# Regrouping nine of sixteen blocks of the last batch during its last pass instead of after it

## What is computed

```python
# per batch b of 8: x is 512 tokens x 2048 features, w = weight[itok[b]] is 2048 x 2048
c = einsum('bsi,boi->bso', x, w)                    # "cond", 4 streams of 512 columns
n = c * rsqrt(mean(c*c) + eps)
H_res  = g * sinkhorn((n @ W_res.T + base) / 0.1, 50 rounds) + (1-g) * I   # 4 x 4 per token
H_pre  = softmax(n @ W_pre.T + base)                # 4 per token
H_post = n @ W_post.T + base                        # 4 per token
y = (sum over j of H_pre[j] * c[stream j]) @ W_branch
out[stream i] = x[stream i] + sum over j of H_res[i, j] * c[stream j] + H_post[i] * y
```

## Time and profile before

| what | value |
|---|---|
| median of 3 runs | 1697.8 us (1697.26 to 1698.08) |
| the profiled execution's own time | 1699.75 us |
| its span | 1698.0 us |
| PE busy | 1685.5 us, 99% of the span |
| DVE busy | 1419.9 us, 84% |
| ACT busy | 717.7 us, 42% |
| POOL busy | 102.5 us, 6% |
| granted clock of TensorE | 1.000 of full speed |
| transfers | 255.55 MB, mean 151 GB/s |

### The profile page before, as it was taken

One profiled execution on the slowest core, in us unless ns is written; L12 is line 12 of the kernel. 1 busy time (PEld: TensorE's weight loads), 2 busy tenths in 40 slices (PEclk: granted clock), 3 DMA queues, 4 the chain that ended last, 5 costly groups with the idle time before them and its releaser, 6 DMA issues.

```text
span 1698.0 us, 24553 instructions
## 1 busy us (share of the span) xinstructions
PE 1685.5 (99%) x7758; PEld 1361.3 (80%) x7758; DVE 1419.9 (84%) x5964; ACT 717.7 (42%) x1171; POOL 102.5 (6%) x143
## 2 busy tenths in 40 slices
PE   9999999999999999999999999999999999999998
PEld 7888788887888878888788878888788877888785
DVE  4322499988999889998899978999799897998798
ACT  4333434244343443444334444334533443335672
POOL 0000000010000100001000000001000010001131
PEclk9999999999999999999999999999999999999999
DMA  6323424376334842448334572346622593227898
GB/s 241 99 88 124 149 88 112 101 216 193 100 100 115 240 166 87 112 130 265 114 95 116 161 249 98 88 126 220 214 88 89 145 300 136 95 92 207 228 217 218
DMA packets 69729, 255.55 MB, mean 151 GB/s; under 512 B 8032, under 2 KB 8160, under 8 KB 68704
## 3 DMA queue, kind: packets, MB, share of 16 engines
q1 hardware_dynamic: 49872, 182.16, 32.7%
q0 software_dynamic: 19728, 71.84, 17.8%
HBM read 204.16 MB, written 45.61 MB: 147 GB/s over the span
## 4 chain that ended last, share of the span: by engine, by line
PE 95%; DMA 2%; DVE 2%; ACT 1%; issue 0%; SPq 0%; DVEq 0%; ACTq 0%
PE acc L1278 79%; PE turn_ps L1315 3%; PE y_ps L1357 3%; PE logit_ps L1323 2%; PE logit_ps L1326 2%; PE acc L1441 1%; DMA w_raw<-wt 1%; PE y_ps L1391 1%; PE acc L1464 1%; PE y_ps L1441 1%; DMA piece<-xn 1%; DVE piece L1127 1%; PE acc L1304 1%; PE turn_ps L1335 0%; PE y_ps L1347 0%; PE acc L1503 0%
## 5 line engine op out<-in xcount | busy, mean ns | idle before, releaser
L1278 PE MATMUL acc<-w_hi,x_hi 128*128 128x512 f32 x2032 | 804.7, 396 | 1.8 <-ACT acc L564 1.8
L1278 PE MATMUL acc<-w_hi,x_lo 128*128 128x512 f32 x2032 | 792.8, 390 | 0.0
L1278 PE MATMUL acc<-w_lo,x_hi 128*128 128x512 f32 x2032 | 791.2, 389 | 0.0
L531 ACT ACTIVATE w_hi<-w_raw 128x1024 fp32r<-128x1024 f32 x255 | 269.2, 1058 | 443.6 <-DMA w_raw<-wt 443.4
L1278 PEld LDWEIGHTS acc<-w_hi,x_hi 128*128 128x128 f32 x2032 | 381.7, 188 | 82.0 <-DVE w_lo L876 2.8
L1278 PEld LDWEIGHTS acc<-w_hi,x_lo 128*128 128x128 f32 x2032 | 381.4, 188 | 81.9
L1278 PEld LDWEIGHTS acc<-w_lo,x_hi 128*128 128x128 f32 x2032 | 382.1, 188 | 76.6
L876 DVE TENSOR_TENSOR w_lo<-w_raw,w_hi 128x1024 fp32r<-128x1024 f32 x256 | 311.9, 1218 | 123.8 <-ACT w_hi L531 114.4
L1127 DVE SCALAR_TENSOR_TENSOR piece<-cond,kern,piece 128x512 f32<-128x512 f32 x408 | 277.6, 748 | 9.2 <-DMA piece<-xn 9.2
L1061 DVE RECIPROCAL vec<-vec 128x8 f32<-128x8 f32 x1536 | 240.4, 198 | 0.0
L1059 DVE TENSOR_REDUCE vec<-work 128x8 f32<-128x32 f32 x1536 | 238.1, 194 | 0.2
(11 more groups left out here) (172 smaller groups left out, 848.8 us busy)
## 6 DMA issues: line engine op xcount, KB each, us to landing
w_raw<-wt SPq DMA_DIRECT2D x255, 512.0 KB, 3.5
x_raw<-xt SPq DMA_DIRECT2D x63, 512.0 KB, 5.6
out<-piece POOLq DMA_DIRECT2D x58, 512.0 KB, 4.8
piece<-xn POOLq DMA_DIRECT2D x56, 512.0 KB, 7.2
out<-cond POOLq DMA_DIRECT2D x12, 512.0 KB, 11.6
grouped<-cond SPq DMA_DIRECT2D x16, 256.0 KB, 9.9
out<-x_raw SPq DMA_DIRECT2D x7, 512.0 KB, 2.6
out<-late_own POOLq DMA_DIRECT2D x6, 512.0 KB, 12.0
```

The lines of the kernel that those rows point to most:

```text
L531: nc.scalar.activation(w_hi[:, unit % HI_SLOTS, :, :], w_raw[:, unit % LO_SLOTS, :, :], ACT.Copy).then_inc(w_hi_ready, 1)
L1278: mm = nc.tensor.matmul(acc[t][:], stationary, moving, start=(chunk == 0 and m == 0), stop=(chunk == CHUNKS - 1 and m == 2))
```

## The change

The 16 transfers are the same in size, source and place. The twelve that concern streams 0 to 2 now go by group of rows. Group 0 is issued once unit 25 is done, group 1 once unit 27 is done, group 2 once unit 29 is done; group 3 and the four transfers of stream 3 stay in the ending. Before the first one SP also waits until stream 2 of the last batch has been copied out of PSUM.

```diff
-            def group_cond(j):
-
-                if j == STREAMS - 1:
-                    sp.wait_ge(cond_ready, BATCHES * STREAMS * TILES)
-                for g in range(GROUPS):
-                    sp.dma_start(grouped[j * GROUP:(j + 1) * GROUP, g, :, :],
-                                 cond[g * GROUP:(g + 1) * GROUP, 1, j, :, :]
-                                 ).then_inc(cond_grouped, 16)
+            def group_cond(j, g):
+
+                sp.dma_start(grouped[j * GROUP:(j + 1) * GROUP, g, :, :],
+                             cond[g * GROUP:(g + 1) * GROUP, 1, j, :, :]
+                             ).then_inc(cond_grouped, 16)
+
+            def group_first_planes(g):
+
+                wait_unit(sp, BATCHES - 1, 3 * PASS_UNITS + 2 * g + 1)
+                if g == 0:
+                    sp.wait_ge(cond_ready, (BATCHES * STREAMS - 1) * TILES)
+                for j in range(STREAMS - 1):
+                    group_cond(j, g)
...
-                for j in range(STREAMS):
-                    group_cond(j)
+                group_first_planes(GROUPS - 1)
+                sp.wait_ge(cond_ready, BATCHES * STREAMS * TILES)
+                for g in range(GROUPS):
+                    group_cond(STREAMS - 1, g)
...
+                    if last and U in range(3 * PASS_UNITS + 2, UNITS, 2):
+                        group_first_planes((U - 3 * PASS_UNITS) // 2 - 1)
```

## The result

| | us, median | lowest to highest | runs |
|---|---|---|---|
| before | 1698.05 | 1697.26 to 1699.05 | 7 |
| the change | 1703.56 | 1702.38 to 1704.86 | 7 |

The change is slower: ratio 1.0033, 95% interval 1.0023 to 1.0043, or +5.5 us. The forecast was no change, with a range to 1700.2 us. The time lies outside it, within 0.3 us of the case that the prediction priced at 1703.3 us and left out.

What follows compares the result with a forecast made beforehand. PE was taken to bound the ending, with no transfer holding it. Terms: 0 (ending) + 0 (SP) + 0 (weights) + 0 (residuals, hidden), so the median stays 1697.8 us; range 1696.8 to 1700.2 us.

Steps and rivals of the forecast that it cites:

- the case that the prediction priced at 1703.3 us and left out: Last pass: all three groups stand wholly before pair 7's residual or the store it hangs on, +5.5 us; outside the range.
- The ending and SP: Ending: removing nine transfers gains 0, PE waits only for ACT. SP: added waits in its queue cost 0.
- How late does the last residual land?: Last pass, pair 7's residual: groups 0 and 1 exceed free DMA time by 3.0 us; VectorE stalls 2.8, hidden, cost 0.
- 2.5 us of cover left: VectorE before the ending: 5.28 us of idle time hides the predicted 2.8 us stall, leaving this much.
- Group 2 was ruled out: Last pass: group 2 is issued after 1578.08 us, too late to pass in front of pair 7's residual; left uncounted.
- Free share: DMA engines in the last pass: share 0.84, so 0.16 x 27.5 = 4.4 us free for the 7.4 us of groups 0 and 1.
- The weights: Unit 30's weights behind group 0 on SP's queue: at worst 3.7 us later, VectorE 0.5 us late, cost 0.
- PE's 7 us of cover: Units 30 and 31: VectorE's weight results are ready 7 us before PE needs each, so cost on the path 0.
- The rule cited: DMA engines alternate between queues per packet, so POOL's transfer waits for one group's packets in turn, not all SP queued; no change.
- Rival 1: Last pass, pair 7's residual outruns VectorE's cover: +1.9 us (two groups) or +5.5 (three); chance 0.13 to +3.4 us, 0.08 beyond.
- margins of 0.25 and 0.2 us: Last pass: residuals of pairs 6 and 7 land this long before VectorE comes to them; any lateness stalls it at once.

Runs made afterwards that it cites:

- group 2 alone: The change with only group 2 issued in the last pass, groups 0 and 1 back in the ending: 1698.46 us against 1698.04 before, ratio 1.0001.
- The runs of two groups: The change with one group back in the ending; early groups 0 and 1: 1698.82 us, 0 and 2: 1699.12, 1 and 2: 1697.74, against 1697.75 before.
- without the residuals: The change without the accumulating residual transfers of pairs 4 to 7 of batch 6: 1698.25 us against 1697.91 before, ratio 1.0000.
- the runs with 128 partitions: The change with each group's 768 KB over 128 partitions: one transfer 1698.05 us against 1697.75 before; three transfers 1697.90 against 1697.91.
- the run of all nine late: Transfers of groups 0 to 2 issued together in the last unit, behind the residual load waiting for unit 30: 1697.37 us against 1698.04 before, ratio 1.0003.
- the repeat: The change itself measured once more, against before on the same chip: 1703.99 us against 1697.91, ratio 1.0038.

## Why the prediction was wrong

**The ending and SP: right.** The ending gains nothing from losing the transfers: its share falls from 1.05 to 0.91 and PE's waits after 1604 us stay at 1.7 us. SP is held nowhere. Where the transfers land does not matter.

**The step that failed: "How late does the last residual land?"** It put 3.0 us, a stall of 2.8, and 2.5 us of cover left. Measured: 9.97 us of waits, and VectorE 5.1 us too late at the ending. Three things in it were wrong.

*One crossing was counted where there are many.* VectorE, the store, ACT's first term, the residual and VectorE again form a ring. A pair's store that starts late lets ACT start late on the pair four further on. The prediction looked at one lap and at the last residual alone. In the change, the waits began at pair 4 with 2.46 us, for which no margin was worked out; weights of unit 30 added 1.60 (predicted 0.5), pair 5 2.37 and pair 7 3.54. ACT, too, waited 8.3 us for stores in the last pass, where it had waited 0.7.

*Group 2 was ruled out by a time that the change itself moves.* "Group 2 goes out only after 1578.08 us ... when the residual of pair 7 has 4 us left to landing" holds only while VectorE is on time, as with group 2 alone. With the lateness of the earlier groups, the residual went out 3.7 us behind group 2. The runs of two groups show the step before that: the residual still led, by 1.1 and 0.4 us, and took 9.6 and 9.5 us to land.

*Free share was taken for free time.* 0.16 x 27.5 us = 4.4 us of free engine time is a mean. In windows of 2 us of the kernel before, the DMA share from 1555 to 1571 us, where groups 0 and 1 are issued, averages 0.92, so 1.3 us are free there; most of the rest lies in a hole right behind:

```profile
1569.00:1571.00 2.00, 2.00 (x12) 1.66 (x11) 2.00 (x3) 1.11 (x3) 0.00 (x0) 1.00 0.92 360
1571.00:1573.00 2.00, 2.00 (x11) 1.65 (x10) 2.00 (x4) 1.77 (x3) 0.97 (x2) 1.00 0.11 43
```

A transfer that lands late because it met a group is late whether or not the engines idle later. One group, 3.7 us alone on the engines by the prediction's estimate, went with a VectorE 5.0 us late (group 0), more than its own length.

**The weights: right in sign, too small, for another reason.** The chain of weights did reach VectorE and did not reach PE. ACT waited 5.8 us for those of unit 30 and rounded them at 1570.12 us; before it was 1565.25, in an execution that stood 2.6 us later, so 7.5 us late where 3.7 had been taken as the worst. The prediction had them wait behind group 0 on their own queue; without the residuals they were not late at all. PE's 7 us of cover held.

**The rule cited.** Turns at the grain of a packet (the Trainium skill, DMA: Bandwidth & Descriptors, "Queues, rings and completion order") were read as a bound: a POOL transfer would not wait for all of SP's queue. The residual of pair 7 took 10.5 us to land where it had taken 7.2, and as it was issued behind group 2, the case that the prediction ruled out was not the one that came. No run here shows the turns themselves; the runs with 128 partitions show that the shape of the transfers mattered, which that reading left out.

**Rival 1** had the place, the threshold (a cover of 5.28 us) and nearly the time: "If all three do, 11.0 - 5.5 = +5.5 us". That it came within 0.3 us is partly luck: the traced loss is 6.4 us, of which 5.1 us are lateness passed on and 1.3 us TensorE's clock, which no term held; and the 11.0 us are not time that three groups take in front of one residual, but stand in for a ring of delays. Its chance beyond 3.4 us, 0.08, was far too low for margins of 0.25 and 0.2 us on a ring of dependent transfers. (The chances do not quite add up either: 0.76 + 0.13 + 0.02 is 0.91 for no change, where 0.90 is stated, and with 0.01, 0.08 and the 0.02 for the unseen the stated ones come to 1.01.)

**What stays open.** Why one group of this shape delays by more than its own length was not measured packet by packet. How far the 5.1 us splits between the stores and the residuals themselves is open too, as is the reason for the wide spread of the two-group runs: that their slower executions had used up the cover is likely and not shown.

## What to carry to other kernels

A transfer moved from an idle place into a busy one is not priced by its bytes over the free share. List every ring of dependent transfers and engines that it passes, with the margin at each step, and let the lateness of one step move the issue times of the next before deciding what it will meet. Moving work earlier has no worth in itself when its reader is 61 us away; here its one effect was to take cover from another chain. Here a copy between 32 partitions crowded out the others far more than the same number of bytes over all 128, so try the other shape before moving such a copy into a busy stretch. And where the time in front of the stretch varies by 3 us, compare the stretch itself.

## What was not expected of the hardware

TensorE's granted clock fell to 0.50, from 2.4 to 1.2 GHz, after it had idled from about 1589 us, and came back to 1.00 in the stretch from 1598 us; a wait of 6.1 us cost 1.3 us more than itself, one of 6.2 us in the repeat 1.6 us more. With 40 small transposes in the wait the clock stayed at 1.00. With three early transfers of 256 KB over 32 partitions VectorE was up to 5.0 us late, with nine over 128 partitions 1.0 us, and 1.2 us before any was issued in the run of all nine late.
